# A four-layer graph and dense network on one core: the last dense layer's weights turned another way, and two graph layers put in another order

## What is computed

```
x = x + L0_gnn(norm(x)); x = x + L0_ffn(norm(x))     # graph layer with similarity; 8 experts, top 2
x = x + L1_gnn(norm(x)); x = x + L1_ffn(norm(x))
x = x + L2_gnn(norm(x)); x = x + L2_ffn(norm(x))     # 4 experts of 2 graph convolutions; 8 experts by a tree
x = x + L3_gnn(norm(x))                              # attention over the edges, then a small dense part
# L3_ffn, the last dense layer:
h      = silu(einsum('td,ehd->teh', xf, w1));  eo = einsum('teh,edh->ted', h, w2)
routed = einsum('te,ted->td', comb, eo)              # comb: weights of the top 2 of 8 experts
shared = silu(xf @ sg_gate.T) * (xf @ sg_up.T) @ sg_down.T
x = x + routed + shared
```

## Time and profile before

| | before |
|---|---|
| median of 3 runs | 644.44 us (642.87 to 645.13) |
| the profiled execution's own time | 646.21 us |
| its span in the profile | 644.5 us |
| PE / DVE / ACT / POOL busy | 93% / 79% / 67% / 17% |

### The profile page before, as it was taken

How to read it: one execution, slowest core, us unless ns; L and a number is a source line. 1 busy time by engine, 2 the same in 40 slices (tenths; PEclk the granted TensorE clock), 3 DMA queues, 4 the chain that set the end, 5 groups by cost and what they waited for, 6 DMA issues and landing times.

```text
span 644.5 us, 9482 instructions
## 1 busy us (share of the span) xinstructions
PE 602.2 (93%) x3100; PEld 489.0 (76%) x3100; DVE 507.1 (79%) x594; ACT 431.0 (67%) x530; POOL 107.0 (17%) x112
## 2 busy tenths in 40 slices
PE   4899999997999999999999999999879689999997
PEld 4676888876688876888888888887768577777776
DVE  6699989874499758888889888898886577777764
ACT  4687787753298669687787877884436566666663
POOL 3100000000000000000000000000347366666630
PEclk9899999999899999999999999999989899999999
DMA  8689999982669767999999999999939699999600
GB/s 256 199 298 306 388 387 378 332 298 72 196 218 353 274 200 247 327 335 342 344 335 335 334 356 335 347 259 217 236 85 228 170 204 257 257 257 257 196 2 17
DMA packets 121233, 168.13 MB, mean 261 GB/s; under 512 B 11259, under 2 KB 49148, under 8 KB 121190
## 3 DMA queue, kind: packets, MB, share of 16 engines
q1 hardware_dynamic: 118884, 165.72, 83.8%
q10 hardware_dynamic: 2322, 2.07, 1.1%
HBM read 167.51 MB, written 0.26 MB: 260 GB/s over the span
## 4 chain that ended last, share of the span: by engine, by line
PE 72%; DVE 13%; ACT 7%; issue 4%; DMA 1%; POOL 1%; ACTq 1%; DVEq 0%; POOLq 0%
PE pre L784 31%; PE y L784 26%; PE tp L796 5%; PE wt L764 4%; DVE w_lo L1189 4%; DVE w_lo L1173 2%; ACT w_hi L495 2%; ACT w_hi L511 2%; PE pre L791 1%; DMA scal<-in_L_gnn_eps 1%; DVE st L1122 1%; POOL rstd L430 1%; ACT L552 1%; ACT h L552 1%; PE pre L976 1%
## 5 line engine op out<-in xcount | busy, mean ns | idle before, releaser
L1189 DVE TENSOR_TENSOR w_lo<-raw,w_hi 128x2048 fp32r<-128x2048 f32 x115 | 259.0, 2287 | 41.3 <-ACT w_hi L511 41.0
L511 ACT ACTIVATE w_hi<-raw 128x2048 fp32r<-128x2048 f32 x116 | 218.3, 1915 | 0.0
L456 POOL TENSOR_TENSOR w_lo<-scratch,w_hi 128x512 fp32r<-128x512 f32 x72 | 91.7, 1295 | 83.3 <-ACT w_hi L491 82.3
L562 ACT ACTIVATE hT_hi<-tp 128x512 fp32r<-128x512 f32 x66 | 39.4, 597 | 93.3 <-PE tp L796 93.3
L784 PE MATMUL y<-w_hi,hT_hi 128*128 128x512 f32 x280 | 85.9, 419 | 0.0
L784 PE MATMUL pre<-w_hi,x_hi 128*128 128x512 f32 x292 | 81.2, 400 | 3.3 <-ACT x_hi L516 2.6
L784 PE MATMUL y<-w_lo,hT_hi 128*128 128x512 f32 x280 | 80.4, 399 | 0.4 <-DVE w_lo L1189 0.4
L784 PE MATMUL pre<-w_lo,x_hi 128*128 128x512 f32 x292 | 79.3, 393 | 1.1 <-DVE w_lo L1189 0.9
L784 PE MATMUL y<-w_hi,hT_lo 128*128 128x512 f32 x280 | 80.3, 399 | 0.0
L784 PE MATMUL pre<-w_hi,x_lo 128*128 128x512 f32 x292 | 78.5, 390 | 0.0
L429 POOL TENSOR_SCALAR rstd<-mv 128x1 f32<-128x1 f32 x11 | 3.3, 304 | 415.0 <-DVE mv L1123 415.0
(11 more groups left out here) (270 smaller groups left out, 667.6 us busy)
## 6 DMA issues: line engine op xcount, KB each, us to landing
raw<-in_L_ffn_w SPq DMA_DIRECT2D x80, 1024.0 KB, 7.2
raw<-in_L_ffn_W SPq DMA_DIRECT2D x32, 1024.0 KB, 10.2
raw<-in_L_ffn_w SPq DMA_DIRECT2D x64, 256.0 KB, 7.7
raw<-in_L_gnn_Wr SPq DMA_DIRECT2D x8, 1024.0 KB, 5.7
raw<-in_L_gnn_Wl SPq DMA_DIRECT2D x8, 1024.0 KB, 6.7
raw<-in_L_gnn_W SPq DMA_DIRECT2D x2, 1024.0 KB, 7.6
raw<-in_L_ffn_sg_gate SPq DMA_DIRECT2D x8, 256.0 KB, 9.6
raw<-in_L_ffn_sg_up SPq DMA_DIRECT2D x2, 1024.0 KB, 13.0
```

What stands on the lines that cost most here:

```text
L456: pool.tensor_tensor(w_lo[:, g % SPLIT_SLOTS, q], w_blocks[:, q], w_hi[:, g % SPLIT_SLOTS, q].bitcast(F32), ALU.subtract).then_inc(blocked ...
L511: act.activation(w_hi[:, g % SPLIT_SLOTS], raw[:, g % RAW_SLOTS], ACT.Copy).then_inc(w_hi_ready, 4)
L562: act.activation(hT_hi[:, (s - 1) % 2], tp[:].rearrange("p (c n) -> p c n", n=P), ACT.Copy).then_inc(hT_hi_ready, 1)
L1189: dve.tensor_tensor(w_lo[:, i], raw[:, g % RAW_SLOTS], w_hi[:, i].bitcast(F32), ALU.subtract).then_inc(w_lo_ready, 4)
```

## The change

In the last dense layer the two ways change places. Gate and up chunks are turned on PE, inside the up product; the 18 down chunks are the blocked ones (`BLOCKED`, `down_chunk`), loaded two at a time in pieces of 256 numbers (1 KB), and go alternately to `scratch` and to `affine`, so that DVE transposes one while the one before is still being rounded and split. Up chunks are loaded in four transfers each, with whole rows, in the order of columns that the blocks of the down chunks need, so x has one form. The second form of x and all that made it are gone. The third chunk is turned ahead of the pipeline too.

In the first graph layer the embedding product comes after two one-hot products in place of five, the small `ab` on ACT after the similarity's exponential, and `normalise_x("l0f")` ahead of the first split. In the third graph layer, the split of the third expert's `agg` moves ahead of the rounding of two chunks, into `aggT[:, 0]`, and the 23 fillers behind it go.

```diff
-FIRST_HOTS = 5
+FIRST_HOTS = 2
+def down_chunk(v):
+    return G_L3F + 2 * v + 5 if v < L3F.n - 2 else G_L3F + 2 * L3F.n + v - (L3F.n - 2)
+BLOCKED = [down_chunk(v) for v in range(L3F.n)]
...
+def raw_slot(g):
+    if blocked(g):
+        v = BLOCKED.index(g)
+        return 2 + 2 * (v // 2 % 2)
+    if g < G_L3F + 2 * L3F.lead:
+        return g % RAW_SLOTS
+    return (6, 7, 0, 1)[((g - G_L3F) // 2 - 2) % 4]
+def agg_slot(e):
+    return 0 if e == 2 else 1
-        w_blocks = scratch[:].rearrange("p (c n) -> p c n", c=KC)
+        w_blocks = [scratch[:].rearrange("p (c n) -> p c n", c=KC), affine]
...
+            def load_up(g, rows, it=None):                     # SP
+                if g < G_L3F + 2 * L3F.lead:
+                    wait_split(sp, g - RAW_SLOTS)
+                else:
+                    sp.wait_ge(w_turned, at(4 * (TURNED.index(g) - 3), 4 * LOOP_TURNED, it))
+                for c in range(KC):
+                    sp.dma_start(raw[:, raw_slot(g), c], rows[c]).then_inc(landed[raw_slot(g)], 16)
+            def load_down(v, columns, it=None):
+                slot = raw_slot(BLOCKED[v])
+                if v < 4:
+                    wait_split(sp, G_L3G + slot - 1)
+                else:
+                    sp.wait_ge(w_blocked, at(4 * (v - 2), 4 * LOOP_BLOCKED, it))
+                for q in range(4):
+                    dst = raw[32 * q:32 * q + 32, slot:slot + 2].rearrange("j s c n -> j (s c n)")
+                    sp.dma_start(dst.rearrange("j (b m) -> j b m", m=2 * P), columns[q]).then_inc(landed[slot], 16)
...
+                def shared_step(s, g, it=None):                # ACT
+                    if s == 0:
+                        activate(s)
+                    turning = G_L3F + 3 if s == 0 else turned_within(g) if s < pipe.n else None
+                    v = s if s == pipe.n - 1 else s - 1
+                    for q in range(4):
+                        if turning is not None:
+                            round_turned_quarter(turning, q, it)
+                        if 0 <= v < pipe.n and s < pipe.n:
+                            round_block(BLOCKED[v], q, it)
+                    if 0 < s < pipe.n:
+                        activate(s, it)
+                    if 1 <= s <= pipe.n:
+                        high_turned(s, it)
...
-            act.wait_ge(sm("scal_in"), 48)                     # ACT, first graph layer: moved
-            act.activation(ab[:], scal[:, 0:2], ACT.Exp).then_inc(sm("ab"), 1)
...
-                    if s == E4:                                # PE, third graph layer
-                        keep_clock(23)
...
-            turn_weights(G_L3F + 3, 0)                         # PE, ahead of L3F
-            turn_weights(G_L3F + 3, 1)
-            keep_clock(25)
+            turn_weights(G_L3F + 1, 1)
+            turn_weights(G_L3F + 1, 2)
+            keep_clock(24)
...
+                    if pipe.lead:                              # DVE, each step of L3F
+                        turning = G_L3F + 3 if s == 0 else turned_within(g) if s < pipe.n else None
+                        for q in range(4):
+                            if turning is not None:
+                                split_turned_quarter(turning, q, it)
+                            if s < pipe.n:
+                                transpose_block(BLOCKED[s], q, it)
...
+            split_turned_quarter(G_L3F + 2, 1)                 # DVE, behind centre_scale("l3g_out")
             dve.wait_ge(sm("rstd"), nth("rstd", "l3g_out"))
```

More of the change, by code:

```diff
@@ L113, in turned_within @@
         return G_L1G
-    return g + AHEAD if g + AHEAD > G_L3F + 3 and turned(g + AHEAD) else None
+    return g + AHEAD if g + AHEAD > G_L3F + 2 and turned(g + AHEAD) else None
+def raw_slot(g):
[5 more added lines that the diff above has]
+    return (6, 7, 0, 1)[((g - G_L3F) // 2 - 2) % 4]
 def rounded(g):
@@ L124, in arrived @@
 def arrived(g):
-    return sum(64 if blocked(c) else 16 for c in range(g % RAW_SLOTS, g + 1, RAW_SLOTS))
+    total = 0
+    for c in range(CHUNKS):
+        if raw_slot(c) == raw_slot(g) and (c <= g) and not (blocked(c) and BLOCKED.index(c) % 2):
+            total += 64 if c >= G_L3F else 16
+    return total
 NORMED = ["l0g", "l0f", "l1g", "l1g_out", "l1f", "l2g", "l2f", "l3g", "l3g_mid", "l3g_out", "l3f"]
@@ L363, in step @@
                     if s < pipe.n:
[L364 to L369, removed]
+                        load(g, w1(s, it), it)
                         g += 1
                     if s >= 2:
[L372 to L375, removed]
+                        load(g, w2(s - 2, it), it)
                 peeled = 8 if pipe.g0 == 0 else 4
@@ L540, in step @@
                             select(1)
[L541 to L543 removed]
+                    if pipe.lead:
+                        shared_step(s, g, it)
                     else:
@@ L1174, in split_turned_quarter, with split_chunk @@
                                   ALU.subtract).then_inc(w_lo_ready, 1)
-            def split_chunk(g, it=None, also=None):
-                if g >= CHUNKS or blocked(g):
+            def split_chunk(g, it=None):
+                if g >= G_L3F:
                     return
@@ L1184, in split_chunk @@
                         split_turned_quarter(g, q, it)
-                        if also is not None and q < 3:
-                            transpose_block(also, q + 1, it)
                 else:
@@ L1229, in step @@
                     g = pipe.chunk(s)
-                    also = g + 4 if blocked(g + 4) else None
+                    if pipe.lead:
+                        turning = G_L3F + 3 if s == 0 else turned_within(g) if s < pipe.n else None
+                        for q in range(4):
+                            if turning is not None:
+                                split_turned_quarter(turning, q, it)
+                            if s < pipe.n:
+                                transpose_block(BLOCKED[s], q, it)
                     if s < pipe.n:
```

241 lines of the change are left out of this document (109 added, 132 removed).

## The result

The changed kernel takes 764.37 us (763.57 to 773.1, 4 runs) against 643.97 us for the one before: 1.188 times as long, 95% interval 1.183 to 1.192. The forecast was 627.5. The kernel before was timed again beside each group of experiments, at 643.7 to 645.7 us, so kernels of different groups are compared by their ratios to it. The profiled execution has a span of 761.8 us. PE's work hardly changed (602.2 us busy before, 612.7 after, some of it at half clock); what it waited for did.

What follows compares the result with a forecast made beforehand. PE was taken as the bound, busy 20.00 of 20.00 us in a first-dense-layer window. The last layer ending at 631.95, with -2.8, -3.1 and +1.5, gave a span of 627.55 and a median of 627.5 us; range 622 to 634.

Steps and rivals of the forecast that it cites:

- the paragraph on transfers: Last layer's loop: up chunk 2.7 us, down chunk 2.7 to 5.0, so 5.4 to 7.7 per step against 7.73, hidden.
- Rival 3: Last layer: down chunks, loaded in pairs in strided pieces, land late; 649 us at 9.4 us per step; chance 0.04.
- 210 against 389 GB/s: Earlier trace's rates for 512 B pieces and whole 2 KB rows, read as speaking against line rate from 512 B up.
- the loop: Last layer, up(4) to up(17): 13 steps of 7.73 us in place of 8.14, -5.3 us.
- rival 1: Last layer's loop isn't freed: a thin margin is missed, the step stays near 8.12 us, 633 us; chance 0.15.
- the head: Last layer, first product to up(4): 35.5 us, with 2.6 us left of the router's wait; -3.7 us.
- the tail: Last layer, up(17) to the end: 15.35 us in place of 18.86, with no turned quarters; -3.5 us.
- the third graph layer: Its end: without fillers and with its own half of `aggT`, the transpose starts 3.09 us earlier; -3.1 us.
- the first: First graph layer: DVE gets the similarity at 12.8 in place of 15.76; -2.8 us, bounds 0 and -3.3.
- rival 2: First graph layer gives nothing, its similarity paced by something hidden behind the wait, such as transfers; 630.3 us; chance 0.06.
- ahead of the last layer: Before the last dense layer: x's transpose waits for the 40 fillers, first product at 480.6 in place of 480.35; +0.25 us.
- PE's clock: Half clock after idle gaps ahead of the fillers and at the router: +1.5 us together, between 0 and 3.4.

Runs made afterwards that it cites:

- the wide kernel: The changed kernel with every up and down transfer of the last layer filling all 128 partitions, down ones in 1 KB pieces, multiplying other numbers: 630.28 us.
- the quarters' kernel: The changed kernel with each up chunk's four transfers filling 32 partitions with four rows each, same bytes to the same places: 640.87 us, 0.994 of before.
- the last kernel: Natural-order up rows, down order 0, 64, 32, 96 and divided fillers (628.67 us), with an up chunk in one 1 MB transfer, not four: 624.1 us, 0.967.
- the kernel with the other down order: The kernel with natural-order up rows (633.77 us), with down transfers issued for partitions 0, 64, 32, 96 in place of 0, 32, 64, 96: 632.25 us, 0.982.

## Why the prediction was wrong

**The step that failed** is the paragraph on transfers, "an up chunk costs 2.7 us", and the verdict "I take it as hidden". The 389 GB/s of the earlier trace rows belong to transfers with 128 rows outermost. I carried the price over to transfers with four blocks outermost because the rows are as long. An up chunk costs 10.9 us (four at 2.7), and the bound on a step became 17.0 us in place of 5.4 to 7.7. The diff showed it (`rows[c]` is 4 x 32 x 512); no row of before did, since no such transfer was in it. Rival 3 had the right place, transfers of the last layer, but a price from down chunks alone: 649 us, at a chance of 0.04.

**A second reading failed too:** 210 against 389 GB/s as small against large pieces. It was 32 against 128 partitions: the wide kernel's 1 KB pieces went at 370 GB/s. So these rows don't speak against the rule on 512 B of the Trainium skill ("DMA: Bandwidth & Descriptors", Specifications), as I had said; the trace agrees with it at 1 KB, and no run tried 512 B into all partitions. With that limit a pair of down chunks costs 9 to 10 us, which is the upper end of the 2.7 to 5.0 that I had given a down chunk, so for these the misreading did little harm: with up rows into 128 partitions the loop came to 8.08 and 7.88 us a step, not quite hidden, but near. Up rows into 32 partitions cost 9.5 us a step together with the down ones (an estimate: 4 MB in two steps at 220 GB/s), and the quarters' loop is bound by transfers. "Below what the window shows with smaller pieces" was no bound at all: the quarters' kernel moved 207 to 225 GB/s.

**The rest, where transfers are out of the way,** can be held against the last kernel:
- the loop: 506.44 to 606.69 in 13 steps is 7.71 each (forecast 7.73). The loss of before, which I had put down to ACT's order, is gone and no quarter is waited for in the loop, so rival 1 is out; no run changed that order alone.
- the head: 506.44 - 471.66 = 34.8 us, forecast 35.5. The wait at the router is 2.14 us, forecast 2.6.
- the tail: 622.0 - 606.69 = 15.3, forecast 15.35. The kernel after has it as well, from 746.52 to 761.8.
- the third graph layer: 57.5 us between its transposes in every kernel with the edit, 60.6 without: -3.1 as forecast. In medians it shows as 1.0 us (interval from 2.6 gained to 0.7 lost).
- the first: similarity at DVE at 13.14, forecast 12.8. But PE's embedding product then starts at 8.7 in some executions and up to 10.5 in others (9.96 before), where it waits for a transfer, as here in the kernel with the other down order:

```profile
9.95 3.75 PE L946 MATMUL pre<-XT,side 128*128 128x128 f32 x16 [1.07 <-DMA side<-in_L_gnn_emb]
```

  This is the wait that takes the place of the old one, a part of rival 2, and the similarity then comes as late as 16.01 (15.76 before). The next transpose of x still comes at 26.1 to 29.7 us in the profiles with the edit, and at 29.7, 30.9 and 31.45 in the three without. Alone the edit gives 2.5 us (0.8 to 4.3), so 2.8 is inside.
- ahead of the last layer: from the layer norm ahead of L3_gnn to the first product of the last layer 43.25 us against 41.44 before, +1.8 and not +0.25; the fillers at half clock are 1.1 of it. The first product still came 7.0 us earlier than in the earlier trace rows, at 473.36, because in this execution the first layer was 4.65 us shorter, the second pair of layers 1.4 and the third graph layer 3.1.
- PE's clock: +1.5 was forecast for the two gaps, each 1.7 or nothing. Ahead of the last layer it cost 1.1 us in the kernel after and nothing in that of the other down order. Behind the router's 2.14 us it stayed at 1.00 in the last kernel and fell in that of the other down order, where the head took 36.35 us and not 34.8:

```profile
504.00:506.00 2.00, 2.00 (x8) 1.63 (x7) 1.89 (x4) 1.20 (x3) 1.17 (x1) 0.50 0.33 123
```

## What to carry to other kernels

Price a transfer by its shape, not by its bytes or by the length of its rows: look at its outermost dimension, since blocks of 4, 8 and 32 or more here showed DMA shares of 0.26, 0.53 and above 1.0, and at the partitions it fills, since transfers into 32 or 64 of them moved at most some 225 GB/s here. When a change recuts a load, look in the trace for a transfer of the same shape; if there is none, the bound is open above, and a rival in which the transfer is several times slower gets a real chance. In the profile, a DMA share of a quarter with an issuing queue that never paused was the mark of a transfer of four blocks; a share of 1.1 with 220 GB/s was that of transfers into 32 or 64 partitions.

## What was not expected of the hardware

- With DMA shares of 0.26, 0.53 and above 1.0, SP's queue took 2.7, 1.4 and 1.0 us for 256 KB; transfers into 64 partitions moved at most 226 GB/s and those into 128 of them 337 to 370, in windows of 4 us.
- One transfer of 1 MB in place of four of 256 KB, with nothing else changed, took the ratio to before from 0.972 to 0.967, some 3 us, which is barely clear of noise.
- PE's clock comes down in stretches that differ from one execution to the next. Between two transposes of x in the second pair of layers the kernels took either 12.8 to 13.2 us, with the clock at 0.50 for a window, or 11.6 with 1.00, whatever had been changed; such events, 1.3 us here and 2.2 in the kernel with the third layer's edit alone, are of the size of a graph layer's gain.
